# A causal attention block: the second pass's mask as a select on GpSimd in place of a mask product on TensorE

## The chip, the cores and the metric

One core of a Trainium2 chip runs the whole kernel. The metric is the device time in microseconds (us). The engines are named as the profile names them: PE is TensorE (matmuls; PEld its weight loads), DVE is VectorE, ACT is ScalarE, POOL is GpSimd, SP issues the transfers.

## The reference

Of the inputs only those of the attention half reach the output: `x` is (4, 2048, 512), and each of the four batches is a sequence of 2048 tokens with 16 heads of 32.

```python
h = _layernorm(x, axis=-1) * (1 + ca) + sa
x = x + ga * _L0_attn_ref(h, ...)
h = _layernorm(x, axis=-1) * (1 + cb) + sb
x = x + gb * _L0_ffn_ref(h, ...)
```

and inside the attention:

```python
att = jnp.einsum('bhqd,bhkd->bhqk', q, k) / jnp.sqrt(jnp.float32(HS))
causal = jnp.tril(jnp.ones((t, t), dtype=bool))[None, None]
att = jnp.where(causal, att, jnp.float32(-1000000000.0))
att = jax.nn.softmax(att, axis=-1)
y = jnp.einsum('bhqk,bhkd->bhqd', att, v)
```

The kernel computes the attention half, its projection and the two normalisations behind it in one launch.

## The kernel before

**Groups.** Four heads make a group (HG = 4), four groups a batch, so 16 groups run one after the other, numbered G = 0 to 15 here. A group begins with the products for q, k and v of the *next* group (L1059, with their rotation on DVE, GpSimd and ScalarE), some 45 us. Then follow 40 steps, some 140 to 185 us, in which the group's attention is computed while the next group's row maxima are found beside it.

**Two passes over the scores.** The first pass (`unit_scores`, L1082) puts scores with queries on the partitions into one of three PSUM banks called `ring`, and DVE reduces each to a row maximum (L843). Its own diagonal mask is a product of `identb` with `mask_qk` (L1085). The second pass (`scores`, L1118) has the keys on the partitions, the maximum already folded into the product, and ScalarE takes the exponential of it (L674) into `prob`. `prob` has three slots, one for each of the last three steps, and `ps_scores` three banks, one for each of the last three heads.

**Steps.** A step is a pair (cq, kt): a chunk of 512 queries and a tile of 128 keys, with kt from 0 to 4 cq + 3. The last four tiles of a chunk are **diagonal steps**: 0 to 3, 8 to 11, 20 to 23 and 36 to 39, of widths 512, 384, 256 and 128 columns. In each of them the first 128 columns of each of four heads need the triangular mask. Before, TensorE adds it to the scores: a second matmul into the same bank, `identb` with `mask_kq` (L1121), 16 steps x 4 heads x 16 groups = 1024 of them.

**What TensorE does in step s, in the order written in its program:** scores of heads 0, 1, 2 of step s with first-pass units between them; then `values` of step s-1 (L1132, product of `prob` with v into `ps_out`); scores of head 3; `denominators` (L1149 of a pair sum, L1155 of one step's `prob`, into `ps_den`); the remaining units; then a projection (L1104) or a head turn, where the step has one. `values` of step s-1 waits until the four exponentials of step s-1 are done. At a group's end there is no step 40, and `values` and `denominators` of step 39 follow directly behind those of step 38.

**What GpSimd does in step s, in order:** the pair sum (L482), two additions of 128x1024 which add `prob` of two successive steps that need no mask, so that one denominator product serves both; then, in some groups, the stages of the previous batch's tail (L500, L512, L452, L454, L524) or of the next batch's head (L452, L454, L473); then the normalisation of a finished chunk (L487) and its low half (L491). GpSimd takes its instructions strictly in this order. Groups differ: G = 0, 1 and 3 have neither tail nor head (called **plain** here), G = 2, 6 and 10 have a head, G = 4, 5, 7, 8, 9, 11, 12, 13 and 14 a tail, and G = 15 projects its own batch and has no next group.

**How many units go into which step** is set by `unit_plan` from the estimated length of each step on TensorE (`product_load`) and DVE (`vector_load`). It knows nothing of the mask.

Of the kernel before, what the change touches and what calls it, by code (L numbers as in the profile page):

```python
# [5 lines left out]
ALU = mybir.AluOpType  # L6
# [6 lines left out]
P = 128  # L13
# [11 lines left out]
def adaln_block_kernel(nc, x, w_qkv, b_qkv, w_proj, b_proj, ln_g, ln_b, c, w_mod, rope_cos, rope_sin, out):  # L25
# [30 lines left out]

    PAIRS = [s for s, (cq, kt) in enumerate(STEPS) if kt < TPC * cq and kt % 2 == 0]
    NP = len(PAIRS)

    LEAVE = {cq: max(i for i, (q, _) in enumerate(STEPS) if q == cq) + 1 for cq in range(NC_ - 1)}  # L60
    LEAVE[NC_ - 1] = -1
# [78 lines left out]
    with ExitStack() as ctx:  # L140
# [35 lines left out]
        ident16 = sb("ident16", [P, P], F16)  # L176
        identb = sb("identb", [P, P], BF16)
        mask_qk = sb("mask_qk", [P, P], BF16)
        mask_kq = sb("mask_kq", [P, P], BF16)
        ones = sb("ones", [P, HS], F32)  # L180
        cT = sb("cT", [P, KC, B], F32)
        eT = sb("eT", [P, KC, B], F32)
# [26 lines left out]
        def tail_buffers(b, t):  # L209
# [37 lines left out]
        max_split, max_turned, max_rows, max_dma = (  # L247
            sem(n) for n in ("max_split", "max_turned", "max_rows", "max_dma"))

        scores_done, exp_done, prob_used, pair_sum, pair_used = (  # L250
            sem(n) for n in ("scores_done", "exp_done", "prob_used", "pair_sum", "pair_used"))

        sums_left, recip_done, out_normed, out_hi, out_split, end_split = (
            sem(n) for n in ("sums_left", "recip_done", "out_normed", "out_hi", "out_split", "end_split"))
# [175 lines left out]
        def _(pool):  # L430
# [2 lines left out]
            pool.memset(ident16[:], 0.0)  # L433
            pool.memset(identb[:], 0.0)
            pool.memset(mask_qk[:], 0.0)
            pool.memset(mask_kq[:], 0.0)
            pool.memset(ones[:], 1.0)
            pool.memset(neg_half[:], -0.5)
            pool.memset(eps_t[:], EPS)
# [1 line left out]
            for one in (ident, ident16, identb):  # L441
# [1 line left out]
                                   pattern=[[-1, P]], channel_multiplier=1)  # L443
            pool.affine_select(out=mask_qk[:], in_=mask_qk[:], compare_op=ALU.is_ge, fill=MASKED, base=0,
                               pattern=[[-1, P]], channel_multiplier=1)
            pool.affine_select(out=mask_kq[:], in_=mask_kq[:], compare_op=ALU.is_ge, fill=MASKED, base=0,
                               pattern=[[1, P]], channel_multiplier=-1)
            pool.drain().then_inc(consts, 1)

            def inv_std(dst, src):  # L450
# [25 lines left out]
            def add_pair(G, j):  # L476

                s = PAIRS[j]
                for p in range(2):
                    pool.wait_ge(exp_done, HG * (NS * G + s + 1) + 2 * p + 2)  # L480
                    pool.wait_ge(pair_used, wait_value(NP * G + j))
                    pool.tensor_tensor(psum2[:, p], prob[:, s % 3, p], prob[:, (s + 1) % 3, p],  # L482
                                       ALU.add).then_inc(pair_sum, 1)

            def out_norm(G, cq):
                pool.wait_ge(recip_done, TPC * (NC_ * G + cq + 1))
# [59 lines left out]
            def body(b, first, last):  # L546
# [3 lines left out]
                for g in range(NG):  # L550
# [9 lines left out]
                    for s in range(NS):  # L560
                        if nxt:
                            n += len(plan[s])
                        if s in tail:
                            uses[tail[s]] = ring_base(b) + n
                        n += (s in tail) + (s in head) + (s in own)
                        if s - 1 in PAIRS and nxt:
                            add_pair(G, PAIRS.index(s - 1))
                        for stage in (0, 1, 3):
                            if s - 2 * stage in tail:
                                t = tail[s - 2 * stage]  # L570
                                job = jobs + t // 2 + (NT // 2 if t >= 2 * T0 and not last else 0)
                                tail_stage(b - 1, t, stage, uses[t], job)
                        if s in own:
                            tail_x(b, own[s], jobs + NT // 2 + own[s] // 2)
                        if s - 1 in own:
                            tail_inverse1(b, own[s - 1])
                        if s - 2 in own:
                            tail_inverse2(b, own[s - 2])
                            pool.drain()
                        if s + 2 in head:  # L580
                            head_tile(b + 1, head[s + 2])
                            pool.drain()
                        if s - 1 in head:
                            head_low(b + 1, head[s - 1])
                        for stage, out_stage in (("norm", out_norm), ("low", out_low)):
                            cq = leaving(s, stage, bool(own))
                            if cq is not None and not (cq == NC_ - 1 and g == 0 and first):
                                out_stage(G - (cq == NC_ - 1), cq)
# [431 lines left out]
        def _(pe):  # L1020
# [88 lines left out]
            def scores(G, par, s, h):  # L1109

                cq, kt = STEPS[s]
                q0 = P * max(kt - TPC * cq, 0)
                w = QC - q0
                diag = kt >= TPC * cq
                k = HG * s + h

                pe.wait_ge(exp_done, wait_value(HG * NS * G + (k - NBK + 1 if k >= NBK else 0)))
                mm = pe.matmul(ps_scores[k % NBK][:, 0:w], qk[0:RM, par, 1, h, kt * P:(kt + 1) * P],  # L1118
                               qk[0:RM, par, 0, h, cq * QC + q0:(cq + 1) * QC], start=True, stop=not diag)
                if diag:  # L1120
                    mm = pe.matmul(ps_scores[k % NBK][:, 0:P], identb[:], mask_kq[:], start=False, stop=True)  # L1121
                mm.then_inc(scores_done, 1)

            def values(G, par, s, paired):

# [2 lines left out]
                if kt == 0:  # L1128
                    pe.wait_ge(sums_left, wait_value(NC_ * G + cq))
                pe.wait_ge(exp_done, HG * (NS * G + s + 1))  # L1130
                for h in range(HG):
                    mm = pe.matmul(ps_out[h * HS:(h + 1) * HS, q0:QC], v32[:, par, kt, h * HS:(h + 1) * HS],  # L1132
                                   prob[:, s % 3, h // 2, h % 2, 0:QC - q0], start=kt == 0,
# [136 lines left out]
```

## Time and profile before

| | |
|---|---|
| median of 3 runs | 3607.25 us (3606.94 to 3612.37) |
| the profiled execution's own time | 3609.68 us |
| its span, first to last instruction | 3607.9 us |
| PE busy | 3197.5 us (89%) |
| DVE busy | 2930.5 us (81%) |
| ACT busy | 1782.1 us (49%) |
| POOL busy | 1709.2 us (47%) |
| mean granted TensorE clock | 0.95 of full |

Busy shares are averages over the whole span. For PE they count each matmul's latency, and these overlap, so the start of the next instruction tells more than a duration. A row of the timeline merges neighbouring instructions of one kind: it gives the start, the length of the whole piece, and their count behind an "x"; in brackets stands the idle time before it and what ended it. The chain of waits follows the work that ended last back through whatever released it.

### The profile page before, as it was taken

The page shows a single profiled execution, that of the slowest core. Times are in us where ns is not written, and L with a number is a line of the kernel's source. Part 1 is how long each engine was busy: PE and PEld are TensorE (multiplying, and loading weights), DVE is VectorE, ACT ScalarE, POOL GpSimd, SP SyncE. Part 2 cuts the span into 40 slices and gives each one's busy share as a digit, 9 for nine tenths or more (in the row PEclk, how much of TensorE's full clock was granted, in tenths as well). Part 3 has the DMA queues.
Part 4 walks back from the last instruction along what each step waited for, and adds up shares of the span by engine and source line. Part 5 has one row for each costly group of instructions (what it writes and reads, how often), then busy time and mean ns, then how long its engine had stood idle before and what let it go on. Part 6 is the DMA issues. An engine that isn't in the chain of part 4 may idle for free.

```text
span 3607.9 us, 62003 instructions
## 1 busy us (share of the span) xinstructions
PE 3197.5 (89%) x22176; PEld 1257.6 (35%) x22176; DVE 2930.5 (81%) x5670; ACT 1782.1 (49%) x3667; POOL 1709.2 (47%) x1385
## 2 busy tenths in 40 slices
PE   3699999999999989989989999989888999999895
PEld 1324343424343332424234243333424334243221
DVE  4797777897778888898888888888888888888667
ACT  3306565555645454564535445465544545444452
POOL 2403435372526455373654636455463554626444
PEclk8759999999999999999999999999999999999897
DMA  6000000110011000110110000011001010001022
GB/s 215 11 12 4 14 11 7 36 36 16 10 39 42 24 24 27 32 40 21 42 53 22 27 30 30 27 33 37 26 30 44 30 36 22 27 19 36 19 91 73
DMA packets 112173, 124.03 MB, mean 34 GB/s; under 512 B 18277, under 2 KB 85093, under 8 KB 110709
## 3 DMA queue, kind: packets, MB, share of 16 engines
q1 hardware_dynamic: 111864, 120.07, 10.4%
q8 instruction: 175, 2.87, 0.3%
q14 instruction: 134, 1.09, 0.1%
HBM read 83.02 MB, written 36.50 MB: 33 GB/s over the span
## 4 chain that ended last, share of the span: by engine, by line
PE 40%; DVE 36%; issue 10%; DVEq 6%; POOLq 2%; ACT 2%; POOL 1%; DMA 0%; SPq 0%; ACTq 0%
DVE mpart L843 11%; PE ring L1082 10%; PE ps_out L1132 9%; PE ps_scores L1118 7%; PE ps_den L1149 4%; DVE qk L820 4%; PE ring L1104 3%; PE ps_den L1155 3%; DVE wk L887 3%; DVE ropeB L828 3%; DVE qk L806 3%; DVE dsum L859 2%; DVE qk L815 2%; PE ps_scores L1059 2%; DVE wk L885 2%
## 5 line engine op out<-in xcount | busy, mean ns | idle before, releaser
L674 ACT ACTIVATE prob<-ps_scores 128x512 f32<-128x512 f32 (+3 forms) x2560 | 1267.5, 538 | 1113.6 <-PE ps_scores L1121 544.4
L843 DVE TENSOR_REDUCE mpart<-ring 128x1 f32<-128x512 f32 (+3 forms) x2560 | 1401.6, 598 | 337.0 <-PE ring L1085 180.4
L482 POOL TENSOR_TENSOR psum<-prob 128x1024 f32<-128x1024 f32 x360 | 868.0, 2432 | 320.6 <-ACT prob L674 160.9
L1082 PE MATMUL ring<-qk 96*128 96x512 f16 (+3 forms) x2560 | 895.7, 370 | 121.7 <-DVE mpart L843 108.9
L1118 PE MATMUL ps_scores<-qk 98*128 98x512 f16 (+3 forms) x2560 | 880.6, 357 | 53.7 <-ACT prob L674 49.6
L1132 PE MATMUL ps_out<-prob,v 128*32 128x512 f32 (+3 forms) x5120 | 609.8, 549 | 4.1 <-ACT qk L634 4.1
L1082 PEld LDWEIGHTS ring<-qk 96*128 96x128 f16 x2560 | 240.4, 99 | 951.1 <-DVE mpart L843 710.1
L1059 PE MATMUL ps_scores<-wg,hT 128*128 128x384 f16 x3072 | 536.7, 327 | 21.4 <-issue 13.6
L464 POOL TENSOR_TENSOR ropeA<-qk,cos_sb 128x256 f32<-128x256 f32 x256 | 198.6, 776 | 741.7 <-DVE v L809 736.8
L1118 PEld LDWEIGHTS ps_scores<-qk 98*128 98x128 f16 x2560 | 249.3, 99 | 360.1 <-ACT prob L674 226.6
L1059 PEld LDWEIGHTS ps_scores<-wg,hT 128*128 128x128 f16 x3072 | 291.7, 98 | 198.1 <-issue 24.2
L629 ACT CAST qk<-qk 128x128 f16<-128x128 f32 x256 | 76.2, 298 | 369.0 <-DVE qk L815 369.0
L859 DVE RECIPROCAL dsum<-dsum 128x128 f32<-128x128 f32 x252 | 234.6, 937 | 19.2 <-ACT osum L701 18.1
L1085 PE MATMUL ring<-mask_qk,identb 128*128 128x128 bf16 x1024 | 234.6, 232 | 0.0
L1121 PE MATMUL ps_scores<-mask_kq,identb 128*128 128x128 bf16 x1024 | 230.9, 227 | 0.0
L1104 PE MATMUL ring<-wp,otin 128*128 128x512 f16 x756 | 186.5, 397 | 41.2 <-DVE mpart L843 28.3
L1155 PE MATMUL ps_den<-prob,ones 128*32 128x512 f32 (+3 forms) x2240 | 219.5, 464 | 0.0
L1149 PE MATMUL ps_den<-psum,ones 128*32 128x512 f32 x1440 | 207.2, 614 | 1.8 <-POOL psum L482 1.8
L512 POOL TENSOR_TENSOR x<-wk,xs 128x512 f32<-128x512 f32 x48 | 61.3, 1276 | 307.7 <-DVE wk L872 307.7
L820 DVE TENSOR_TENSOR qk<-qk 128x128 f16<-128x128 f32 x256 | 179.2, 700 | 1.2
L452 POOL TENSOR_TENSOR vare<-mv,eps_t 128x1 f32<-128x1 f32 x192 | 54.3, 283 | 256.6 <-DVE mv L717 86.9
L806 DVE SCALAR_TENSOR_TENSOR qk<-ps_scores,bg 128x256 f32<-128x256 f32 x256 | 108.7, 424 | 81.8 <-PE ps_scores L1059 48.6
(127 smaller groups left out, 3142.4 us busy)
## 6 DMA issues: line engine op xcount, KB each, us to landing
xs<-in_L_attn_x_dram SPq DMA_DIRECT2D x124, 256.0 KB, 2.7
attn_out_T<-ot SPq DMA_DIRECT2D x63, 256.0 KB, 2.1
otin<-attn_out_T SPq DMA_DIRECT2D x30, 512.0 KB, 4.5
out_dram<-x SPq DMA_DIRECT2D x60, 256.0 KB, 2.1
wg<-w_qkv_halves SPq DMA_DIRECT2D x16, 768.0 KB, 5.2
qk<-in_L_wmod_dram SPq DMA_DIRECT2D x1, 6144.0 KB, 27.1
bc<-modulation SPq DMA_DIRECT2D x4, 1536.0 KB, 8.9
hT<-in_L_attn_W_qkv_dram SPq DMA_DIRECT2D x1, 3072.0 KB, 10.7
```

Source lines behind the costliest of these rows:

```text
L482: pool.tensor_tensor(psum2[:, p], prob[:, s % 3, p], prob[:, (s + 1) % 3, p], ALU.add).then_inc(pair_sum, 1)
L674: act.activation(prob[:, s % 3, p, h % 2, 0:w], ps_scores[(HG * s + h) % NBK][:, 0:w], ACT.Exp, scale=SCALE).then_inc(exp_done, 1)
L820: dve.tensor_tensor(qk16[:, u, :, 2 * HS:3 * HS], ropeR[:, u, :, 0, :], qk16[:, u, :, 0:HS], ALU.subtract)
L843: dve.tensor_reduce(mpart[:, h, qt, kc:kc + 1], ring[n % NBK][:, 0:w], AX.X, ALU.max).then_inc(ring_free, 1)
L859: dve.reciprocal(dsum[:, cols], dsum[:, cols]).then_inc(recip_done, 1)
L1059: mm = pe.matmul(ps_scores[(t + SHIFT) % NBK][:, 0:GW], hT[:, a, k, t * P:(t + 1) * P], wg[:, g % 2, w, k, :], start=(i == 0), stop=(i == ...
L1082: mm = pe.matmul(ring[n % NBK][:, 0:w], qk[0:R, par, 0, h, qt * P:(qt + 1) * P], qk[0:R, par, 1, h, kc * QC:kc * QC + w], start=True, stop ...
L1104: mm = pe.matmul(ring[n % NBK][:, :], att, wp16[:, w, k, :], start=(i == 0), stop=(i == 3 * NG - 1))
L1118: mm = pe.matmul(ps_scores[k % NBK][:, 0:w], qk[0:RM, par, 1, h, kt * P:(kt + 1) * P], qk[0:RM, par, 0, h, cq * QC + q0:(cq + 1) * QC], st ...
L1132: mm = pe.matmul(ps_out[h * HS:(h + 1) * HS, q0:QC], v32[:, par, kt, h * HS:(h + 1) * HS], prob[:, s % 3, h // 2, h % 2, 0:QC - q0], start ...
L1149: mm = pe.matmul(ps_den[h * HS:(h + 1) * HS, :], ones[:], psum2[:, h // 2, h % 2, :], start=kt == 2, stop=False)
L1155: mm = pe.matmul(ps_den[h * HS:(h + 1) * HS, q0:QC], ones[:], prob[:, s % 3, h // 2, h % 2, 0:QC - q0], start=kt == 0, stop=kt == TPC * (c ...
```

## The change

The mask product of the second pass and its constant `mask_kq` are left out, so the exponential is taken of unmasked scores. GpSimd then replaces the wrong entries of the first 128 columns of each head in `prob` by zero, one select per diagonal step over the four heads: 128 partitions x (4 x 128) f32 elements, in place, 16 x 16 = 256 selects in all. In GpSimd's program it stands behind the pair sum and ahead of the tail, head and normalisation work of the step. It waits for the fourth exponential of its step; `values` of a diagonal step waits for the select as well, by a new semaphore `diag_masked`, and `denominators` stands behind `values`.

```diff
--- before
+++ after
+    DIAGS = [s for s, (cq, kt) in enumerate(STEPS) if kt >= TPC * cq]
...
-        mask_kq = sb("mask_kq", [P, P], BF16)
...
-            pool.affine_select(out=mask_kq[:], in_=mask_kq[:], compare_op=ALU.is_ge, fill=MASKED, base=0,
-                               pattern=[[1, P]], channel_multiplier=-1)
...
+            def mask_diagonal(G, s):
+
+                block = prob[:, s % 3].rearrange("p a h q -> p (a h) q")[:, :, 0:P]
+                pool.wait_ge(exp_done, HG * (NS * G + s + 1))
+                pool.affine_select(out=block, in_=block, compare_op=ALU.is_ge, fill=0.0, base=0,
+                                   pattern=[[0, HG], [1, P]], channel_multiplier=-1).then_inc(diag_masked, 1)
...
                         if s - 1 in PAIRS and nxt:
                             add_pair(G, PAIRS.index(s - 1))
+                        if s in DIAGS:
+                            mask_diagonal(G, s)
                         for stage in (0, 1, 3):
...
-                diag = kt >= TPC * cq
...
-                mm = pe.matmul(ps_scores[k % NBK][:, 0:w], qk[0:RM, par, 1, h, kt * P:(kt + 1) * P],
-                               qk[0:RM, par, 0, h, cq * QC + q0:(cq + 1) * QC], start=True, stop=not diag)
-                if diag:
-                    mm = pe.matmul(ps_scores[k % NBK][:, 0:P], identb[:], mask_kq[:], start=False, stop=True)
-                mm.then_inc(scores_done, 1)
+                pe.matmul(ps_scores[k % NBK][:, 0:w], qk[0:RM, par, 1, h, kt * P:(kt + 1) * P],
+                          qk[0:RM, par, 0, h, cq * QC + q0:(cq + 1) * QC], start=True, stop=True).then_inc(scores_done, 1)
...
                 pe.wait_ge(exp_done, HG * (NS * G + s + 1))
+                if s in DIAGS:
+                    pe.wait_ge(diag_masked, len(DIAGS) * G + DIAGS.index(s) + 1)
```

TensorE, first group, steps 8 and 9 (second pass of width 384, then the `values` of step 8). Before:

```order
L1118 MATMUL ps_scores<-qk 128x384 [waits exp_done]
L1121 MATMUL ps_scores<-mask_kq,identb 128x128
L1132 MATMUL ps_out<-prob,v 32x512 [waits exp_done]
L1132 MATMUL ps_out<-prob,v 32x512 x3
L1082 MATMUL ring<-qk 128x256 [waits ring_free]
L1085 MATMUL ring<-mask_qk,identb 128x128
L1118 MATMUL ps_scores<-qk 128x384 [waits exp_done]
L1121 MATMUL ps_scores<-mask_kq,identb 128x128
L1149 MATMUL ps_den<-psum,ones 32x512 [waits pair_sum]
```

After, the same place:

```order
L1124 MATMUL ps_scores<-qk 128x384 [waits exp_done]
L1137 MATMUL ps_out<-prob,v 32x512 [waits diag_masked,exp_done]
L1137 MATMUL ps_out<-prob,v 32x512 x3
L1089 MATMUL ring<-qk 128x256 [waits ring_free]
L1092 MATMUL ring<-mask_qk,identb 128x128
L1124 MATMUL ps_scores<-qk 128x384 [waits exp_done]
L1154 MATMUL ps_den<-psum,ones 32x512 [waits pair_sum]
```

The mask products are gone, and the first `values` product has the wait on the select; units, scores and denominators stand behind it as before.

GpSimd, first group, the steps from 4 on (pair sums, the normalisation of chunk 0 and its low half, pair sums of chunk 2). Before:

```order
L482 TENSOR_TENSOR psum<-prob 128x1024 [waits pair_used,exp_done] x4
L487 TENSOR_TENSOR osum<-osum,dsum 128x512 [waits recip_done]
L491 TENSOR_TENSOR ot<-osum,ot 128x512 [waits out_hi]
L482 TENSOR_TENSOR psum<-prob 128x1024 [waits pair_used,exp_done] x4
L487 TENSOR_TENSOR osum<-osum,dsum 128x512 [waits recip_done]
```

After:

```order
L480 TENSOR_TENSOR psum<-prob 128x1024 [waits pair_used,exp_done] x4
L487 AFFINE_SELECT prob<-prob 128x4x128 [waits exp_done]
L492 TENSOR_TENSOR osum<-osum,dsum 128x512 [waits recip_done]
L487 AFFINE_SELECT prob<-prob 128x4x128 [waits exp_done] x2
L496 TENSOR_TENSOR ot<-osum,ot 128x512 [waits out_hi]
L487 AFFINE_SELECT prob<-prob 128x4x128 [waits exp_done]
L480 TENSOR_TENSOR psum<-prob 128x1024 [waits pair_used,exp_done] x4
```

Step 8's select stands directly behind a pair sum, the next ones between the normalisation and its low half, and step 11's behind that low half.

## Rows read from the trace of the kernel before

**Rows 1.** The page: chain of waits by engine, and two groups of instructions.
```profile
PE 40%; DVE 36%; issue 10%; DVEq 6%; POOLq 2%; ACT 2%; POOL 1%; DMA 0%; SPq 0%; ACTq 0%
...
L482 POOL TENSOR_TENSOR psum<-prob 128x1024 f32<-128x1024 f32 x360 | 868.0, 2432 | 320.6 <-ACT prob L674 160.9
L1121 PE MATMUL ps_scores<-mask_kq,identb 128*128 128x128 bf16 x1024 | 230.9, 227 | 0.0
```
**Rows 2.** The chain of waits by line, stretch 514 to 531 us (plain group).
```profile
by line: PE ring L1082 24.4%; PE ps_out L1132 21.8%; PE ps_den L1155 15.4%; PE ps_scores L1118 14.9%; PE ps_den L1149 5.9%; DVE mpart L843 4.1%; PE ps_scores L1121 4.1%; ACT prob L674 3.8%; ACT osum L701 2.7%; ACT dsum L700 2.5%; PE ring L1
```
**Rows 3.** The chain of waits by line, stretch 1358 to 1378 us (tail group).
```profile
by line: PE ring L1082 18.9%; DVE mpart L843 16.8%; DVE wk L887 13.5%; PE ps_den L1155 11.1%; DVE wk L885 6.9%; PE ps_out L1132 6.8%; PE ps_den L1149 5.0%; DVEq L932 4.5%; PE ps_scores L1118 4.2%; issue 3.8%; DVE wk L931 3.3%; PE ps_scores 
```
**Rows 4.** Timeline of ACT, PE and POOL, group 5, step 22: end of step 21 on.
```profile
1369.23 0.27 PE L1118 MATMUL ps_scores<-qk 98*128 98x256 f16 x1
1369.35 0.22 PE L1121 MATMUL ps_scores<-mask_kq,identb 128*128 128x128 bf16 x1
...
1369.60 0.38 ACT L674 ACTIVATE prob<-ps_scores 128x256 f32<-128x256 f32 x1 [0.89 <-PE ps_scores L1121]
...
1371.25 0.22 PE L1118 MATMUL ps_scores<-qk 98*128 98x128 f16 x1
1371.31 0.22 PE L1121 MATMUL ps_scores<-mask_kq,identb 128*128 128x128 bf16 x1
...
1372.05 0.64 PE L1132 MATMUL ps_out<-prob,v 128*32 128x256 f32 x8
```
**Rows 5.** Timeline of POOL at the kernel's start: memsets and selects; then one addition.
```profile
1.29 0.20 POOL L436 MEMSET mask_kq<- 128x128 bf16 x1
...
1.52 0.10 POOL L439 MEMSET eps_t<- 128x1 f32 x1
1.91 0.54 POOL L442 TENSOR_SCALAR_AFFINE_SELECT ident<-ident 128x128 f32<-128x128 f32 x2 [0.29 <-issue]
...
1309.91 1.27 POOL L500 TENSOR_TENSOR xs<-xs,bc 128x512 f32<-128x512 f32 x1
```
**Rows 6.** Timeline, group 1, steps 8 and 9 (plain group).
```profile
513.00 4.67 POOL L482 TENSOR_TENSOR psum<-prob 128x1024 f32<-128x1024 f32 x2 [2.39 <-PE ps_den L1149]
...
515.95 1.36 ACT L674 ACTIVATE prob<-ps_scores 128x512 f32<-128x512 f32 x3 [0.90 <-PE ps_scores L1121]
...
516.95 1.07 PE L1132 MATMUL ps_out<-prob,v 128*32 128x512 f32 x8
```
**Rows 7.** Timeline, group 5, steps 20 and 21 (tail group).
```profile
1357.79 5.13 POOL L482 TENSOR_TENSOR psum<-prob 128x1024 f32<-128x1024 f32 x2
...
1360.78 2.69 DVE L887 SCALAR_TENSOR_TENSOR wk<-wk,rstd,bc 128x512 f32<-128x512 f32 x1
...
1361.06 1.07 PE L1132 MATMUL ps_out<-prob,v 128*32 128x512 f32 x8
...
1364.16 0.39 PE L1082 MATMUL ring<-qk 96*128 96x512 f16 x1 [2.04 <-DVE mpart L843]
```
**Rows 8.** Timeline, group 5, steps 11 and 12 (tail group).
```profile
1326.14 1.16 POOL L491 TENSOR_TENSOR ot<-osum,ot 128x512 f16<-128x512 f32 x1 [0.16 <-issue]
...
1327.02 0.43 PE L1132 MATMUL ps_out<-prob,v 128*32 128x128 f32 x8
...
1328.66 0.75 DVE L887 SCALAR_TENSOR_TENSOR wk<-wk,rstd,bc 128x512 f32<-128x512 f32 x1
```
**Rows 9.** Timeline, end of group 1: steps 38 and 39, then the next group's products.
```profile
624.28 0.28 ACT L674 ACTIVATE prob<-ps_scores 128x128 f32<-128x128 f32 x1 [0.51 <-PE ps_scores L1121]
624.63 0.41 PE L1132 MATMUL ps_out<-prob,v 128*32 128x128 f32 x8
...
626.49 4.06 PE L1059 MATMUL ps_scores<-wg,hT 128*128 128x384 f16 x24 [1.24 <-issue]
```
**Rows 10.** Timeline of PE, start of group 5: one form before, in and after a low clock.
```profile
1276.69 0.39 PE L1118 MATMUL ps_scores<-qk 98*128 98x512 f16 x1 [2.26 <-ACT prob L674]
1277.44 0.53 PE L1118 MATMUL ps_scores<-qk 98*128 98x384 f16 x1
...
1280.85 0.33 PE L1118 MATMUL ps_scores<-qk 98*128 98x384 f16 x1
```
**Rows 11.** Windows view, 1277 to 1281 us: lengths and busy us by engine, granted clock.
```profile
1277.00:1281.00 4.00, 3.72 (x31) 2.78 (x30) 0.91 (x3) 4.00 (x8) 0.00 (x0) 0.57 0.02 6
```

More of the change, by code:

```diff
@@ L248, in adaln_block_kernel @@
             sem(n) for n in ("max_split", "max_turned", "max_rows", "max_dma"))
-        scores_done, exp_done, prob_used, pair_sum, pair_used = (
-            sem(n) for n in ("scores_done", "exp_done", "prob_used", "pair_sum", "pair_used"))
+        scores_done, exp_done, diag_masked, prob_used, pair_sum, pair_used = (
+            sem(n) for n in ("scores_done", "exp_done", "diag_masked", "prob_used", "pair_sum", "pair_used"))
         sums_left, recip_done, out_normed, out_hi, out_split, end_split = (
@@ L435, in _ @@
             pool.memset(mask_qk[:], 0.0)
-            pool.memset(mask_kq[:], 0.0)
             pool.memset(ones[:], 1.0)
```

## Prediction

> **What bounds the kernel now.** I read the chain of waits first, since busy shares mislead here. It stands 40% on TensorE, 36% on DVE, with another 6% in DVE's queue [rows 1]. Neither engine alone sets the end, so a term counts only where its engine is on the chain. Then I asked which it is around the diagonal steps. In a plain group nearly all named parts are PE: 24.4 + 21.8 + 15.4 + 14.9 + 5.9 + 4.1 = 86.5% [rows 2]. In a tail group the PE lines named make 18.9 + 11.1 + 6.8 + 5.0 + 4.2 = 46%, and DVE lines take about the same [rows 3]. Last I laid the select into the timeline, step by step, and read what GpSimd was doing when a step's exponentials ended.
>
> **What is removed.** The page gives the mask product 230.9 us for 1024 instructions, 227 ns each [rows 1]. That is latency. The cost is what the next instruction is held back: scores start at 1369.23, the mask at 1369.35; and where the scores are as narrow as the mask, 1371.25 and 1371.31, so 128 columns hold the array 0.06 us [rows 4]; unrounded starts give 0.056. So 4 x 0.056 = 0.22 us a diagonal step, 1024 x 0.056 = 57 us in all. Weight loads run beside matmuls and add nothing. With PE on the chain for 46% to 87% of these stretches, I count 60%: **-34 us** (ends 0 and -57).
>
> The Trainium skill, TensorE: Matmul & The Clock Gate, Back-to-back issue gap, gives two figures for such a stream: an isolated spacing of about 56 ns at 128 columns, and about 81 ns where weight loads and matmuls alternate. Its second figure would make the whole removal 83 us, 50 at my 60%; the trace's alternating stream has the first.
>
> **What is added on GpSimd.** No select of 512 elements is in the trace. The 128-column one takes 0.54 us for two, 0.29 each by its record; a memset of one column 0.10, of 128 columns 0.20 [rows 5]. Fixed part 0.10, the rest in proportion: 0.10 + 4 x 0.19 = **0.87 us**. Low end: the extra 384 columns at the memset's pace, 0.29 + 384 x 0.0008 = 0.6; high end four whole selects, 1.17. A two-input addition of 512 takes 1.27 [rows 5], and a one-input operation should not exceed it. I take 0.87, nearest to the row of the same operation. 256 of them are 223 us on an engine busy 47% of the time. The work itself hides; its place in the queue need not.
>
> **What is added on TensorE: a wait.** Behind the waiting `values` stand head 3 of the scores, hence ScalarE, the denominators, and the units, hence DVE. A select ends at the later of the last exponential and GpSimd's previous instruction, plus 0.87, plus 0.1 us for each of two signals.
>
> Where it hides: step 22 of group 5. The fourth exponential of that step ends at 1369.60 + 0.38 = 1369.98, `values` starts at 1372.05 [rows 4]: 2.07 us of cover against 1.07. The reason is TensorE's order: denominators, units and three scores lie between. Of 256 diagonal steps some 175 are like this.
>
> Where it doesn't (sums over groups, same reading):
> - Step 8 of the six groups without a tail. GpSimd adds a pair until 513.00 + 4.67 = 517.67, the exponentials of the step ended at 516.55, `values` began at 516.95 [rows 6]. The select ends 518.54; the wait is 1.7 us, 10.5 in six groups. TensorE is on the chain: all counts.
> - Step 20, the same pair sum: until 1362.92, with `values` at 1361.06 [rows 7], a wait of 2.6 to 2.9 in six tail groups, 0.9 to 1.9 in the six others; 22.8 in sum. In the tail groups TensorE sits idle 2.04 us until 1364.16 for DVE anyway [rows 7], and only what goes beyond, some 0.9, counts: 6 x 0.9 + 6.9 = 12.3.
> - Step 36, pair sum again: 0.1 to 1.3 us, 8.1 in all, on the chain.
> - Step 39. With no step 40, nothing covers it: last exponential at 624.28 + 0.28 = 624.56, `values` at 624.63 [rows 9], a wait of 1.0. It is 0.5 where scores come later, and 2.9 in group 15 with GpSimd in the tail. 13.4 in all, on the chain, since the next group's products follow.
> - Step 11 of tail groups: the select stands behind L491, which ends 1327.30; `values` was at 1327.02 [rows 8]. 1.6 or 1.1 each, 12.9 in nine groups. The chain is DVE there, which has units in its banks; I count 2.
> - Step 3, 0.3 to 0.5 in ten groups: 4, of which 2.
> All together 73 us of waits (53 with a 0.6 us select, 107 with 1.17), of which 10.5 + 12.3 + 8.1 + 13.4 + 2 + 2 = **+48 us** on the chain.
>
> **The clock.** At the start of group 5, after TensorE waited 2.26 us, 384 columns take 0.53 us, later 0.33 [rows 10]; the granted clock over that stretch averages 0.57 [rows 11], mostly the 1.2 GHz level. The new waits of 1 to 2.9 us are of that kind, and each mask product gone leaves less work between them. If some 16 of them draw a low stretch like this one, which costs up to 2 us of delayed work, that is at most 32; half the time something else binds or the clock holds: **+12** (0 to 30).
>
> **DVE beside GpSimd.** L887 takes 0.75 us with GpSimd idle [rows 8] and 2.69 us inside a pair sum [rows 7]. Rows do not say whether a one-input select does the same. A select meets such an operation rarely: **+5** (0 to 25).
>
> The Trainium skill, GPSIMD Engine Reference, Specifications, says that the engine shares its SBUF interfaces with VectorE and collides with instructions in a two-port mode or with two SBUF inputs. By it the selects would stretch such DVE operations too, a rule against this change; the 0.75 and 2.69 us agree for additions.
>
> **Sum.** -34 + 48 + 12 + 5 = +31 us. Against the profiled execution: 3609.7 + 31 = 3641; the median lies 2.4 lower, so 3638, said as 3640 us.
>
> **Rivals.**
> 1. *The waits are absorbed.* DVE's three banks hold about 2 us of reductions, so short waits of TensorE might cost nothing beyond step 39 and a part of the pair-sum steps. Then 48 becomes 20, clock and contention nothing: 3607 - 34 + 20 = 3593, down to 3580 with a 0.6 us select. For it: 36% of the chain on DVE. Against it: the largest waits fall in plain groups, where PE is the chain. This is the faster side. It decides below about 30 us of counted waits.
> 2. *A wash*: gain about equal to waits, 3600 to 3614. For it: both terms live in the same steps.
> 3. *The select is dear* (1.2 us or more, slowed by DVE as DVE is by it). Then the cover in steps 9, 10 and 23, which is 1.1 to 1.9 us, is gone too: waits 107 or more, 73 of them counted at the same two thirds, clock 30, contention 15: 3607 - 34 + 73 + 30 + 15 = 3691, up to 3715.
> 4. *The mask doesn't leave the path*: were scores held by the exponentials and not by their own length, dropping 0.06 us gives nothing, the gain is 10 and the result 3607 - 10 + 48 + 12 + 5 = 3662. That is inside the forecast's range.
>
> **Chances.** Forecast with rival 4, 3615 to 3685: 0.55. Rival 1: 0.20. Wash: 0.12. Rival 3: 0.13. A measurement of this kernel can tell about 0.2% (7 us) from no change: faster 0.20, same 0.12, slower 0.68. The range leaves out the far parts of rivals 1 and 3: 3588 to 3705.
>
> **What would show it.** The select's mean duration near 0.87 us, 256 of them. TensorE's waits at `values` for the select: near 73 us in all, none at step 22, 1.7 at step 8 of plain groups, 1.0 at step 39. Every group should be longer by 1 to 3 us. The L1121 rows should be gone, PE busy down by some 230 us though the time is not. Wrong would be: selects above 1.2 us, waits at most diagonal steps, or a span of plain groups shorter than before, which would say that the waits were absorbed.

## The result and the profile after

| | before | after |
|---|---|---|
| median | 3607.10 us (3605.69 to 3612.37, 4 runs) | 3642.72 us (3639.88 to 3646.11, 4 runs) |
| ratio, 95% interval | | 1.0096 (1.0079 to 1.0114) |
| profiled execution | 3609.68 us | 3643.34 us |
| span | 3607.9 us | 3641.6 us |
| PE busy | 3197.5 us | 3171.3 us |
| POOL busy | 1709.2 us | 1872.1 us |
| mean granted TensorE clock | 0.950 | 0.945 |

The changed kernel is about 1% slower, 35.6 us. Beside a second set of runs of before it gave 1.0105 (1.0091 to 1.0119). In the profile of the changed kernel, `values` is L1137, the second pass's scores L1124, the first pass's L1089, the exponential L681, the pair sum L480, the select L487.

Page of the changed kernel: the chain of waits by engine, then groups of instructions (busy us, mean ns of one, idle before with its main releaser). They answer to [rows 1].

```profile
DVE 35%; PE 32%; issue 9%; POOL 8%; DVEq 6%; ACT 4%; POOLq 3%; DMA 1%; SPq 0%; ACTq 0%
...
L480 POOL TENSOR_TENSOR psum<-prob 128x1024 f32<-128x1024 f32 x360 | 868.1, 2432 | 252.4 <-PE ps_den L1154 158.2
...
L1137 PE MATMUL ps_out<-prob,v 128*32 128x512 f32 (+3 forms) x5120 | 616.0, 553 | 69.3 <-POOL prob L487 44.8
...
L487 POOL TENSOR_SCALAR_AFFINE_SELECT prob<-prob 128x512 f32<-128x512 f32 x256 | 168.2, 657 | 519.6 <-ACT prob L681 518.5
```

GpSimd was 1% of the chain and is now 8%, TensorE was 40% and is 32%. The chain's new GpSimd part is mostly not the selects but the pair sums that they queue behind: the page gives `POOL psum L480` 5% of the span. TensorE's idle time before `values` was 4.1 us in all and is 69.3, 44.8 of it put down to the select. One select takes 0.66 us in the mean. Summed over the groups, TensorE's idle time before `values` is 2.4 us at step 3, 10.2 at step 8, 7.6 at 11, 22.5 at 20, 8.0 at 36 and 8.5 at 39: 59 of the 73 us that were forecast.

Timeline, group 1, step 8 (plain group), to be read against [rows 6]; the pair sum of 520.12 is the second of its two additions:

```profile
520.12 2.35 POOL L480 TENSOR_TENSOR psum<-prob 128x1024 f32<-128x1024 f32 x1
520.52 1.36 ACT L681 ACTIVATE prob<-ps_scores 128x512 f32<-128x512 f32 x3 [0.73 <-PE ps_scores L1124]
...
522.41 0.63 POOL L487 TENSOR_SCALAR_AFFINE_SELECT prob<-prob 128x512 f32<-128x512 f32 x1
...
523.20 1.94 PE L1137 MATMUL ps_out<-prob,v 128*32 128x512 f32 x8 [1.69 <-ACT prob L681]
```

The exponentials are done at 521.1, the addition holds GpSimd until 522.4, and TensorE idles 1.69 us. (The row names ACT as releaser, a neighbour of the real one: the select ends at 523.04, `values` starts at 523.20.)

The same for group 5, step 20 (tail group), against [rows 7]:

```profile
1377.54 5.11 POOL L480 TENSOR_TENSOR psum<-prob 128x1024 f32<-128x1024 f32 x2
...
1380.52 2.67 DVE L894 SCALAR_TENSOR_TENSOR wk<-wk,rstd,bc 128x512 f32<-128x512 f32 x1
...
1382.60 1.09 POOL L487 TENSOR_SCALAR_AFFINE_SELECT prob<-prob 128x512 f32<-128x512 f32 x1
...
1383.84 1.94 PE L1137 MATMUL ps_out<-prob,v 128*32 128x512 f32 x8 [2.91 <-POOL prob L487]
```

A select beside a DVE operation with two SBUF inputs takes 1.09 us here in place of 0.63; 12 of the 256 take over 0.8. And both `values` after a wait take 1.94 us for eight matmuls where they took 1.07 [rows 6, 7]: TensorE is at half clock. That is not so everywhere: of the six groups that wait 1.7 us at step 8, only group 1 shows it in this trace; behind the 2.9 us waits of step 20 all six tail groups are at the low clock for part of the interval that follows. That is looked at below.

The end of group 1, against [rows 9]:

```profile
632.28 0.28 ACT L681 ACTIVATE prob<-ps_scores 128x128 f32<-128x128 f32 x1 [0.45 <-PE ps_scores L1124]
632.62 0.64 POOL L487 TENSOR_SCALAR_AFFINE_SELECT prob<-prob 128x512 f32<-128x512 f32 x1 [2.44 <-ACT prob L681]
...
633.40 0.43 PE L1137 MATMUL ps_out<-prob,v 128*32 128x128 f32 x8 [0.59 <-POOL prob L487]
```

Here nothing queues on GpSimd, and TensorE still waits: `values` comes 0.84 us after the last exponential, where it came 0.07 after it.

**Where the time went, by place.** I took the starts of `values` of all 640 steps in both traces and the difference of each interval. In the five intervals that end in `values` of steps 8, 11, 20, 36 and 39, summed over the groups, the changed kernel is longer by 9.5, 12.1, 21.8, 9.3 and 11.1 us, 63.8 together. All other intervals within the groups are shorter by 24.1 in sum (most by 0.1 to 0.2 us where a diagonal step is in them), the 15 changes of group by 3.7. The rest is at the two ends. By group, from `values` of step 0 to that of the next group, the changed kernel is up to 6.5 us longer, but groups 8, 11, 12 and 14 are 1.1 to 3.6 us shorter (group 15 has no next one).

### The profile page after: what moved, and what is told of

Same layout as the page of the kernel before. It is cut to its first block, busy times and chain, and to the rows that moved or that the text cites. A ratio compares the mean times of both kernels' runs of the same rounds, so it can differ in the third digit from the quotient of the medians.

```text
span 3641.6 us, 60464 instructions
## 1 busy us (share of the span) xinstructions
PE 3171.3 (87%) x21152; PEld 1194.3 (33%) x21152; DVE 2923.3 (80%) x5670; ACT 1777.0 (49%) x3667; POOL 1872.1 (51%) x1639
## 3 DMA queue, kind: packets, MB, share of 16 engines
q1 hardware_dynamic: 111864, 120.07, 10.4%
## 4 chain that ended last, share of the span: by engine, by line
DVE 35%; PE 32%; issue 9%; POOL 8%; DVEq 6%; ACT 4%; POOLq 3%; DMA 1%; SPq 0%; ACTq 0%
DVE mpart L850 11%; PE ps_out L1137 8%; PE ring L1089 7%; PE ps_scores L1124 5%; POOL psum L480 5%; DVE qk L827 4%; PE ps_den L1154 4%; DVE ropeB L835 3%; PE ring L1111 3%; DVE qk L813 3%; PE ps_den L1160 2%; ACT prob L681 2%; DVE qk L822 2%; DVE wk L894 2%; PE ps_scores L1066 2%
## 5 line engine op out<-in xcount | busy, mean ns | idle before, releaser
L681 ACT ACTIVATE prob<-ps_scores 128x512 f32<-128x512 f32 (+3 forms) x2560 | 1262.0, 539 | 1144.9 <-PE ps_scores L1124 1071.1
L1089 PE MATMUL ring<-qk 96*128 96x512 f16 (+3 forms) x2560 | 893.6, 370 | 123.1 <-DVE mpart L850 104.5
L480 POOL TENSOR_TENSOR psum<-prob 128x1024 f32<-128x1024 f32 x360 | 868.1, 2432 | 252.4 <-PE ps_den L1154 158.2
L1124 PE MATMUL ps_scores<-qk 98*128 98x512 f16 (+3 forms) x2560 | 877.4, 358 | 42.7 <-ACT prob L681 38.7
L1137 PE MATMUL ps_out<-prob,v 128*32 128x512 f32 (+3 forms) x5120 | 616.0, 553 | 69.3 <-POOL prob L487 44.8
L1089 PEld LDWEIGHTS ring<-qk 96*128 96x128 f16 x2560 | 241.5, 99 | 976.1 <-DVE mpart L850 743.3
L487 POOL TENSOR_SCALAR_AFFINE_SELECT prob<-prob 128x512 f32<-128x512 f32 x256 | 168.2, 657 | 519.6 <-ACT prob L681 518.5
L1124 PEld LDWEIGHTS ps_scores<-qk 98*128 98x128 f16 x2560 | 247.8, 99 | 355.5 <-ACT prob L681 218.4
L866 DVE RECIPROCAL dsum<-dsum 128x128 f32<-128x128 f32 x252 | 234.8, 937 | 21.8 <-ACT osum L708 20.7
L1154 PE MATMUL ps_den<-psum,ones 128*32 128x512 f32 x1440 | 212.6, 629 | 1.8 <-POOL psum L480 1.8
L1137 PEld LDWEIGHTS ps_out<-prob,v 128*32 128x32 f32 x5120 | 103.8, 108 | 275.2 <-ACT prob L681 153.1
L835 DVE TENSOR_TENSOR ropeB<-qk,sin_sb 128x256 f32<-128x256 f32 x256 | 121.3, 474 | 24.0 <-issue 0.4
## 6 DMA issues: line engine op xcount, KB each, us to landing
hT<-in_L_attn_W_qkv_dram SPq DMA_DIRECT2D x1, 3072.0 KB, 10.4
```

The costliest lines, as they stand in the source:

```text
L681: act.activation(prob[:, s % 3, p, h % 2, 0:w], ps_scores[(HG * s + h) % NBK][:, 0:w], ACT.Exp, scale=SCALE).then_inc(exp_done, 1)
L1089: mm = pe.matmul(ring[n % NBK][:, 0:w], qk[0:R, par, 0, h, qt * P:(qt + 1) * P], qk[0:R, par, 1, h, kc * QC:kc * QC + w], start=True, stop ...
L1154: mm = pe.matmul(ps_den[h * HS:(h + 1) * HS, :], ones[:], psum2[:, h // 2, h % 2, :], start=kt == 2, stop=False)
```

## Experiments

Each kernel is named by its label. "Products" are the second pass's mask products on TensorE. Ratios are to runs of the kernel before on the same chip, with 95% intervals. Except in experiment 10 the edits shown are against the changed kernel, with lines left out at "..."; `selected(G, s)` says where a select stands, and `masked` is true where the product is kept.

**1. The removal alone** (`e1_no_mask`).

```diff
-                        if s in DIAGS:
+                        if selected(G, s):
                             mask_diagonal(G, s)
...
-                if s in DIAGS:
-                    pe.wait_ge(diag_masked, len(DIAGS) * G + DIAGS.index(s) + 1)
+                if selected(G, s):
+                    pe.wait_ge(diag_masked, selects_to(G, s))
```

Here `selected` is never true.

> Leaves the second pass's causal mask out altogether: no mask product, no select, no wait on one; its output is not the reference's. It prices the removal alone. Theory of the prediction (1024 x 0.056 = 57 us of TensorE, of which 60% on the chain): 34 us faster than before, 3573. If the steps between selects in the changed kernel are typical (each only 0.1 to 0.2 us shorter, where 0.22 is the whole), 20 to 35 us faster. Rival, scores held by exponentials, so that the removal gives nothing: within 10 us of before.

Measured: 3584.46 us, 0.9929 (0.9916 to 0.9941), **25.5 us faster**. Of the 57 us that the products hold the array, 45% counts. The 34 us of the prediction were too many; the removal does give time.

**2. The addition alone** (`e2_both`).

```diff
+                if masked:
+                    mm = pe.matmul(ps_scores[k % NBK][:, 0:P], identb[:], mask_kq[:], start=False, stop=True)
```

Here `masked` is true in all diagonal steps, and selects and waits stay as in the changed kernel.

> Keeps the mask product and adds the select and the wait of values on it. It prices the addition alone. If removal and addition add up, this is before plus (36 plus what the run without any mask gains): 3607 + 36 + 34 = 3677 by the prediction's gain. By the prediction's own terms for the addition (48 waits + 12 clock + 5 contention = 65) 3672, less some 15 for a select of 0.66 us in place of 0.87. Rival, waits absorbed: below 3630.

Measured: 3647.96 us, 1.0103 (1.0089 to 1.0117), **38 us slower**. The two parts do not add up: -25.5 + 38 = +12.5, and the whole change measured +36. Beside selects, taking all products out gains next to nothing (1.0103 against 1.0096 and 1.0105). Some 23 us (the intervals leave it at 15 to 31) are neither in the one part nor in the other. By the starts of `values` in the profiled executions, about 7 of them lie in the five intervals named above, 5 in the others within the groups and 8 at the changes of group.

**3. GpSimd's work without the wait** (`e3_select_elsewhere`).

```diff
-                block = prob[:, s % 3].rearrange("p a h q -> p (a h) q")[:, :, 0:P]
+                block = scratch[:]
...
-                if s in DIAGS:
-                    pe.wait_ge(diag_masked, len(DIAGS) * G + DIAGS.index(s) + 1)
```

> Keeps the mask product; GpSimd does its selects at the same 256 places behind the same wait for the exponentials, but as two of 256 elements each on a tile of their own, for which nobody waits. It prices GpSimd's time, its later tail and head work and any slowing of DVE, without TensorE's wait. Prediction: contention 5 us and late GpSimd work nothing, so 3607 to 3615. Rival, selects slow DVE as additions do or delay tail and head work: 3625 or more.

Measured: 3604.00 us, 0.9983 (0.9975 to 0.9992). Two half selects take 0.90 us here (0.452 each), more than one whole. So 230 us of added GpSimd work cost nothing; the kernel is even 6 us *faster*. The loss comes with TensorE's wait, and what surrounds it. (The scratch tile is bf16, where `prob` is f32, so this run need not price the contention with DVE exactly.) The gain has its own reason (experiment 10).

That a select does stretch DVE shows in the traces. The same DVE operation with GpSimd idle, before, and with nothing but a select beside it, in the changed kernel:

```profile
1439.06 0.75 DVE L933 SCALAR_TENSOR_TENSOR x<-wk,rstd,xs 128x512 f32<-128x512 f32 x1
```

```profile
1244.85 0.69 POOL L487 TENSOR_SCALAR_AFFINE_SELECT prob<-prob 128x512 f32<-128x512 f32 x1 [3.93 <-ACT prob L681]
1245.12 0.96 DVE L940 SCALAR_TENSOR_TENSOR x<-wk,rstd,xs 128x512 f32<-128x512 f32 x1
```

Nine such operations take 0.96 us, 0.21 more than alone: about 2 us in all.

**4. Selects only where they are covered** (`e4_covered`), and **5. more of them** (`e8_more_covered`).

```diff
+    def selected(G, s):
+        return s in DIAGS and (s in (0, 1, 9, 10, 21, 22, 37, 38) and G < 15)
...
+    def product_masked(G, s):
+        return s in DIAGS and (not (s in (0, 1, 9, 10, 21, 22, 37, 38) and G < 15))
```

> Selects only in steps 0, 1, 9, 10, 21, 22, 37 and 38 of groups 0 to 14, where the last exponential is out long before values starts; mask products in all other diagonal steps. If the loss comes from the few places where GpSimd is busy or nothing covers the select, this one is faster than before: 8 steps x 15 groups x 0.22 = 26 us of TensorE, 60% of it: 3591 (3581 to 3602). If each select costs wherever it stands, slower than before: 3607 + 18 = 3625.

Measured: 3593.59 us, 0.9956 (0.9942 to 0.9969), 16 us faster than before. That looks like the middle of what the covered places should give, but it is not: the selects in steps 0 and 1 also delay an addition of the tail groups, and the changes of group are 10.0 us shorter in this trace, as in experiment 10, which has no select at all. Against that kernel (0.9971) the covered selects give about 5 us. The second version adds steps 2 and 23, step 8 of the tail groups and step 20 of groups 7, 11 and 14.

> The eight covered steps of before in groups 0 to 14, and with them steps 2 and 23 there, step 8 of the groups with a tail, step 20 of groups 7, 11 and 14: 162 selects in place of 120. By cover alone faster than the version with 120: 42 x 0.22 = 9 us of TensorE, some 5 on the chain, ratio 0.994 to before. Rival: the cover of steps 2 and 23 in plain groups is a few tenths only, and DVE sets the pace in the tail groups' added steps: no better than 0.9956.

Measured: 3586.02 us, **0.9935 (0.9923 to 0.9947)**, 24 us faster than before, with 162 of 256 selects. It is as fast as leaving the mask out altogether, but for another reason: its changes of group are 10.3 us shorter, those of experiment 1 only 2.3. Against experiment 10 the selects give about 13 us. TensorE's idle time before `values` is 4.5 us in all, where it was 4.1. It is the best complete version of this study. Its page:

```profile
span 3583.5 us, 61032 instructions
...
PE 3167.0 (88%) x21528; PEld 1208.6 (34%) x21528; DVE 2923.8 (82%) x5670; ACT 1776.2 (50%) x3667; POOL 1810.8 (51%) x1547
...
L1154 PE MATMUL ps_out<-prob,v 128*32 128x512 f32 (+3 forms) x5120 | 614.9, 553 | 4.5 <-ACT qk L654 3.9
...
L500 POOL TENSOR_SCALAR_AFFINE_SELECT prob<-prob 128x512 f32<-128x512 f32 x162 | 104.2, 643 | 418.4 <-ACT prob L694 417.2
```

**6. Selects only where they are not covered** (`e5_uncovered`): `selected` is `s in (3, 8, 11, 20, 36, 39)`, products elsewhere.

> Selects only in steps 3, 8, 11, 20, 36 and 39 of every group, the places where the changed kernel's trace shows TensorE waiting; mask products elsewhere. If the places are independent, it is the changed kernel without the gain of the covered ones: 1.0096 over 0.9956, 1.014, so 3660 (3652 to 3668). If the loss were a matter of how many selects there are, 96 of 256, it would be 0.4 of the 1.03% that selects beside kept products cost: 3622.

Measured: 3642.86 us, 1.0089 (1.0075 to 1.0103), 33 us slower. The 96 badly placed selects make nearly the whole loss of the changed kernel, so the place decides and not the number. But 3660 was expected. With experiment 4 that is +33 - 16 = +17, where the whole is +36: again some 19 us appear only when both are together.

**7. One cause at a time**: step 39 alone (`e6_only_39`, `selected` is `s == 39`) and the steps behind a pair sum (`e7_only_8_20_36`).

> Selects only in step 39 of every group, 16 in all; mask products elsewhere. Reading of both traces: step 39 is 11 us longer in sum over the groups, and the next group's products follow, so before plus 10: 3620 (3615 to 3623). Rival, ScalarE's two copies and the next group's start absorb it: within 4 us of before.

Measured: 3613.85 us, 1.0015 (1.0006 to 1.0024), 5 us slower by the ratio and 3.7 by the medians. Its profiled execution, with 3620.33 us (span 3618.6) the second longest of eleven, has the interval before step 39 longer by 9.5 us. Sixteen selects cost 0.1% to 0.2%: less than the 10 us expected, and whether under the rival's 4 the interval leaves open.

> Selects only in steps 8, 20 and 36, which come right behind a pair sum in GpSimd's queue; mask products elsewhere. From the steps' lengths in the two traces 9.5 + 21.8 + 9.3 = 41 us, less a few given back later: 3645 (3636 to 3652). By the prediction's count, in which DVE's own lateness absorbs two thirds of the wait in step 20 of tail groups: 10.5 + 12.3 + 8.1 = 31, so 3638 or less with the shorter select. The step's own length in tail groups tells which: 2.8 us longer, or 0.9.

Measured: 3627.43 us, 1.0054 (1.0042 to 1.0067), 19 us slower, where 38 were expected and 31 by the prediction's count. The intervals before steps 8, 20 and 36 are longer by 10.4, 22.4 and 9.0 us, as in the changed kernel. But the interval behind step 20 is *shorter* by 13.9 in sum, 1.7 to 3.3 in each of the six tail groups. Its timeline, group 5 (its `values` is L1154, first-pass scores L1102, the denominators of a pair L1171):

```profile
1375.67 1.08 POOL L500 TENSOR_SCALAR_AFFINE_SELECT prob<-prob 128x512 f32<-128x512 f32 x1
...
1376.90 1.07 PE L1154 MATMUL ps_out<-prob,v 128*32 128x512 f32 x8 [2.83 <-POOL prob L500]
1377.90 0.39 PE L1102 MATMUL ring<-qk 96*128 96x512 f16 x1
...
1378.44 1.07 PE L1171 MATMUL ps_den<-psum,ones 128*32 128x512 f32 x8
```

TensorE waits 2.83 us before `values`, and right behind it the unit starts without a wait, where it stood 2.04 us before [rows 7]. In this group 2.1 of the 2.8 us are given back; the prediction had two thirds. (Some of the 13.9 is not the wait's: in experiments 1, 4, 5 and 10, with no wait there, this interval is 3.4 to 4.7 us shorter too.) In the changed kernel the same interval gives back 2.5 us in all and not 13.9. The difference between the two goes with the clock: here eight matmuls take 1.07 us, there 1.94. In the six traces in which tail groups wait at step 20 for a select behind the pair sum, this interval lasts 5.06 us wherever its granted clock is 1.00 (8 of 36 times), 6.3 to 6.7 at 0.74 to 0.76 and 7.7 to 7.9 at 0.60 to 0.63.

**The clock.** Windows view of the changed kernel, group 5, from before step 20 on; columns are length, busy us of PE, PEld, DVE, ACT, POOL, granted clock, DMA share and GB/s:

```profile
1378.00:1384.00 6.00, 3.09 (x25) 1.19 (x27) 5.85 (x7) 2.87 (x7) 5.69 (x3) 0.93 0.58 175
1384.00:1388.00 4.00, 4.00 (x18) 0.56 (x17) 1.45 (x3) 0.49 (x1) 0.63 (x1) 0.50 0.02 6
1388.00:1392.00 4.00, 3.87 (x23) 0.88 (x19) 1.45 (x3) 0.88 (x3) 0.00 (x0) 0.74 0.00 0
1392.00:1396.00 4.00, 3.78 (x35) 1.07 (x27) 3.93 (x8) 1.44 (x5) 1.38 (x3) 1.00 0.00 0
```

And of `e2_both`, the same place with the products kept:

```profile
1376.00:1382.00 6.00, 3.33 (x29) 1.39 (x30) 5.85 (x7) 2.76 (x6) 5.52 (x3) 1.00 0.56 175
1382.00:1386.00 4.00, 4.00 (x33) 1.20 (x26) 1.79 (x4) 0.61 (x2) 0.64 (x1) 1.00 0.01 2
1386.00:1390.00 4.00, 3.99 (x33) 1.32 (x30) 3.93 (x9) 1.69 (x5) 1.13 (x3) 1.00 0.02 4
```

Behind the wait of step 20 the changed kernel runs at 1.2 GHz (0.50) for more than 4 us, just when it has work to catch up on; with products kept it is at 2.4 GHz in this group. Group 5 flatters the comparison, though. In the interval behind step 20 the six tail groups are all below full clock in the changed kernel (0.61 to 0.76), four of them in `e2_both` too (4, 8, 9 and 12, 0.62 to 0.74), one in `e7_only_8_20_36` (0.74), and three before, with no wait for a select at all (0.79 to 0.80). The mean granted clock of the profiled executions: 0.950 before and in experiment 1, 0.949 and 0.950 in 4 and 5, 0.948 in 6 (0.949 to 0.952 in its other three executions), 0.953 in experiment 10, 0.952 in experiment 3, `e2_both` and `e7_only_8_20_36`, but 0.945 and 0.946 in the changed kernel (0.944 to 0.946 in its first four executions). Taking 1 minus the clock, doubled, times the span as time at the low level gives 401 us after, 361 before and 350 in `e2_both`. The 50 us between the last two cost at most half, 25 us, of TensorE's time: the size of what does not add up in experiment 2. But most of them, some 41, lie at the changes of group (86 against 45 us at the low level), and experiment 1 has 81 there though its changes of group are 2.3 us shorter than before. So the low clock there need not cost anything, and it is not shown that the clock is what does not add up. Between before and after it is 40 us, so at most 20.

**8. What draws the low clock** (`e11_products_kept`): selects and waits everywhere, `product_masked` is `s in (3, 8, 11, 20, 36, 39)`; beside it the changed kernel again (`after_again`).

> The changed kernel, selects and waits in all diagonal steps, with the mask product kept as well in steps 3, 8, 11, 20, 36 and 39, where TensorE waits for the select anyway (the product changes nothing in the output there). It adds 96 x 4 x 0.056 = 21 us of TensorE work. Theory, that taking the products out next to the waits gains nothing and lets the clock fall: no slower than the changed kernel and more likely 5 to 15 us faster, 3628 to 3643, with fewer low stretches than its 253 us. Rival, that the granted clock is a matter of chance and the product costs what it holds the array: 3650 or more.

> The changed kernel again, beside the run with products kept, on the same chip: ratio 1.0096 to before as the first time, 3643 (3639 to 3648), mean granted clock 0.945 against 0.950.

Measured: 3650.19 us, 1.0113 (1.0097 to 1.0128), and 3645.78 us, 1.0105 (1.0091 to 1.0119). My theory fell: products kept at the waits neither save time nor lift the clock, which stays at 0.945. What is known then: with all products kept the clock is 0.952, with those of the other, covered steps gone it is 0.945, and going from the one to the other (`e2_both` to `e11_products_kept`) gains nothing. Without waits, taking 120 of those 160 steps' products out (experiment 10 to experiment 4) lowered the clock as well, from 0.953 to 0.949, and gained about 5 us. The lowest clocks stand where there are both waits and less work. Why the covered steps' products count and those at the waits don't, and how much of the 23 us of experiment 2 is the clock's, no run here settles.

**9. The order on GpSimd** (`e9_select_first`).

```diff
+                        if selected(G, s + 1) and s - 1 in PAIRS and nxt:
+                            mask_diagonal(G, s + 1)
                         if s - 1 in PAIRS and nxt:
                             add_pair(G, PAIRS.index(s - 1))
-                        if s in DIAGS:
+                        if selected(G, s) and not (s - 2 in PAIRS and nxt):
                             mask_diagonal(G, s)
```

> The changed kernel with one order turned around on GpSimd: in steps 8, 20 and 36 the select stands ahead of the pair sum. Theory, that the conflict is inherent: the select is on time, but the pair sum ends some 3 us later and the denominators wait for it, 45 times 2 to 4 us in place of 41 us: slower than the changed kernel, 3690 or more. Rival, that the pair sum has slack of its own (its denominators come a step later): those 41 us gone, 3605.

Measured: 3718.50 us, 1.0305 (1.0291 to 1.0319), 110 us slower. Timeline, group 1, steps 8 and 9 (its select is L500, pair sum L493, exponential L696, pair denominators L1173):

```profile
522.11 0.64 POOL L500 TENSOR_SCALAR_AFFINE_SELECT prob<-prob 128x512 f32<-128x512 f32 x1 [5.79 <-ACT prob L696]
522.72 4.66 POOL L493 TENSOR_TENSOR psum<-prob 128x1024 f32<-128x1024 f32 x2
...
525.18 0.87 ACT L696 ACTIVATE prob<-ps_scores 128x384 f32<-128x384 f32 x2 [3.14 <-POOL psum L493]
526.00 2.50 PE L1173 MATMUL ps_den<-psum,ones 128*32 128x512 f32 x6
```

The wait of `values` shrinks, and ScalarE, which may not overwrite `prob` before the pair sum has read it, waits 3.14 us in its place. The interval behind step 8 alone is longer by 50 us in sum. In neither of the two orders are both on time there; a select between the two additions of a pair sum was not tried.

**10. Why GpSimd's added work saved 6 us** (`e10_tail_waits`), made on the kernel before:

```diff
                             add_pair(G, PAIRS.index(s - 1))
+                        if s == 2 and s in tail:
+                            pool.wait_ge(exp_done, HG * (NS * G + s + 1))
```

> The kernel before with one wait more and nothing else: in step 2 of groups with a tail, GpSimd waits for that step's last exponential before the tail's first addition, as it does behind a select. Theory: the addition no longer meets the rotation on DVE at the group's start (longest product there 1.32 us before, 0.94 in all runs with a select ahead of it), 9 groups x 0.9 to 1.2 = 8 to 10 us faster, 3600. Rival, that the addition is needed early: slower.

Measured: 3598.31 us, 0.9971 (0.9959 to 0.9982), **11 us faster** from one wait. Before, in group 5:

```profile
1272.40 1.31 POOL L500 TENSOR_TENSOR xs<-xs,bc 128x512 f32<-128x512 f32 x1 [0.16 <-issue]
1272.68 1.31 DVE L828 TENSOR_TENSOR ropeB<-qk,sin_sb 128x256 f32<-128x256 f32 x1
```

With the wait, the same product, the last of group 5 (L830 there):

```profile
1268.88 0.42 DVE L830 TENSOR_TENSOR ropeB<-qk,sin_sb 128x256 f32<-128x256 f32 x1
```

GpSimd used to start the tail's first addition as soon as it was free, 17 us before anyone needed it, and beside it DVE's rotation product took 1.31 us in place of 0.42, in the one stretch where the next group's transposes wait for it. All nine such products go from 1.31 to 0.42 us, and the changes of group before the nine tail groups are shorter by 8.4 us in sum (all fifteen by 9.3). A select in step 0, 1 or 2 waits for an exponential as this added wait does, and the versions with such selects have this gain: these nine changes are 9.2 us shorter in experiment 3 and 7.8 in the changed kernel. In experiments 1, 6 and 7, where no select stands ahead of that addition, the fifteen changes are at most 2.3 us shorter.

## Why the prediction was right, point by point

- **The result**, 3640 against 3642.7 measured, is nearer than the terms deserve, and that is luck: two large errors cancelled. The removal, put at -34, gives 0 to 3 us beside selects, and the additions, put at 65 (48 + 12 + 5), cost 38 (44 against experiment 3). The forecast of 1 to 3 us more in every group failed: the first fifteen lie between 3.6 us shorter and 6.5 longer.
- **Removal, -34**: measured alone -25.5 (experiment 1). The term that failed is the share on the chain, 60%, which was read off two stretches [rows 2, 3]: alone it is 45%, and beside selects it is next to nothing, which no term foresaw. The 0.056 us a product holds: 1024 x 0.056 = 57 us is the most that can go, and PE busy, which was forecast to fall by some 230 us, fell by only 26.2 on the page though the 230.9 us of L1121 are gone, which I take to be because matmuls overlap in the records and the low clock stretches those that are left; no run separates the two.
- **The select, 0.87 us** (0.6 to 1.17): 0.66 in the mean, near the low end. Scaling everything above the fixed part by the columns was wrong; the extra columns cost the memset's pace, about 0.9 ns each ((635 - 292) / 384), against 1.5 assumed. The bound at the low end, 0.29 + 384 x 0.0008, has the mechanism.
- **The waits, +48**: `e2_both` is +38 and contains 10 us of the unforeseen gain of experiment 10, so +48 for waits, clock and all, where the sum had 65. Two errors within it go opposite ways: the selects are shorter, and the first count of step 11, 2 of 12.9 us on the chain, was too low; its interval is longer by 12.1, of which 3.2 also stand in experiment 1, and the second interval behind it gives back 4. (The six sizes listed add up to 71.7 and not 73, and by its own rows step 11 of group 5 waits 1.2 to 1.4 us, which is neither its 1.6 nor its 1.1.) The places were right, 8, 11, 20, 36 and 39, and so were the sizes at most of them, taken as lengths of the intervals: 10.5 forecast and 9.5 found at step 8, 22.8 and 21.8 at step 20, 8.1 and 9.3 at step 36, 13.4 and 11.1 at step 39. Step 22 and its like are covered.
- **Absorption at step 20 of tail groups**, 0.9 of 2.6: right where the clock holds (`e7_only_8_20_36`, 5.06 us for the interval behind), wrong in the changed kernel, where that interval takes 6.3 to 7.9 us at the low clock.
- **The clock, +12**: the mean fell from 0.950 to 0.945, at most 20 us. The 12 lies within that bound; it was not measured. Waits alone do not lower the mean (`e2_both` 0.952, experiment 3 without them 0.952); taking work out lowers it without waits (0.953 to 0.949) and more with them (0.952 to 0.945).
- **Contention, +5**: nothing is lost in the total (experiment 3, with a bf16 tile). A select is itself stretched to 1.09 us beside L894, and it does stretch DVE, 0.75 to 0.96 us in nine operations of the changed kernel, which is less than the term.
- **Rival 1**, absorbed waits, and the **wash** are out by experiment 2, **rival 3** by the 0.66 us. **Rival 4**, a removal that gives nothing, is wrong for the removal alone and right in its number, by a mechanism that stays open, for the removal beside selects.

## What to carry to other kernels

Work that moves to a half-idle engine was free here only where that engine's *queue* was empty when its input was ready and the one who waits came later anyway: lay the new instruction into the trace at every place where it will run, and convert only the places with cover. Here that turns a change of +1% into one of -0.65%, of which about 0.36% is the selects' own and the rest comes from the delayed addition. A matmul's profile duration is no price; start to start is the most that its removal can give, and here 45% of it came. And an addition nobody waits for can cost a neighbour: delaying it until it is needed gained 0.3%.

## What I had not expected of the hardware

- The parts of a change did not add: -25.5 and +38 us made +36. The granted clock went 0.950 and 0.952 in the parts, 0.945 in the whole, and in group 5 matmuls right behind a wait of 2.7 to 2.9 us ran at 1.2 GHz for more than 4 us (0.50 in the window 1384 to 1388) in one version and at 2.4 GHz in the other. Which groups fall differs from version to version; the cause is open.
- A one-input select of 512 f32 elements per partition takes 0.63 us on GpSimd where an addition of that size takes 1.27 [rows 5], and up to 1.09 beside a DVE operation with two SBUF inputs. The slowing is mutual: 0.75 to 0.96 us for such a DVE operation beside one select.
- One GpSimd addition of 1.31 us stretched a DVE product from 0.42 to 1.31 us, and avoiding nine such meetings gained 11 us of 3609, 8.4 of them at the nine changes of group.
